# A two-layer transformer on one core: input loads on separate semaphores, and query stacks loaded from ScalarE's queue

## The chip, the cores and the metric

One Trainium2 chip; the program runs on one core. The engines are TensorE (PE in the profile), VectorE (DVE), ScalarE (ACT), GpSimd (POOL) and SyncE (SP), which only issues DMAs here. The metric is the device time of one execution in microseconds. The profile's span leaves out what lies before its first and after its last instruction.

## What is computed

x is 4 batches of 512 tokens with 128 features. Four blocks follow each other, each with a layer norm of x ahead of it and its result added to x:

```
x = x + attention0(layernorm(x))   # 16 heads of 8; low-rank q and kv projections; rotary part added
x = x + layers(layernorm(x))       # 6 layers of windowed attention (16 heads of 64, window 32) and a gated FFN
x = x + attention1(layernorm(x))   # 16 heads of 8; rotary
x = x + experts(layernorm(x))      # top-1 of 16 experts, capacity 160
```

Both attentions are full softmax over 512 keys for each of 16 heads and 4 batches, in float32 precision: queries and keys are split into three bfloat16 parts (high, middle, low), and one matmul over 48 rows of such parts gives a product of float32 accuracy.

## The kernel before

The program is written engine by engine: each engine has its own list of instructions, and semaphores order them. A wait stops all that is behind it on its engine. `LOADED` is 16 for each load counted by `ld_c`.

**Inputs.** SP issues `ident` and x (L411, L412, semaphore `ld_x`), and then in a loop (L413, L414) nine constants and four weights, all counted by `ld_c`: `mean_w`, the rope tables (512 KB each), the rotary tables of the layers, the two masks, `moe_c`, `upper`, `packed`, `packed_low`, the bias columns and `gate_t`. TensorE transposes x (L655), ScalarE copies it to `xT` (L1248), and all three of TensorE, ScalarE and VectorE then wait for the full count of `ld_c` (L657, L1249, L1540). VectorE copies the masks to bfloat16 (L1542, L1543), and sets `tick` (L1546), for which the first mean waits through `step_done`.

**Opening of an attention** (`attention(a)` of each engine, a is 0 or 1). For batches 0 and 1: mean by a matmul (L295), centring (L1444), squares (L1141), variance (L673), root (L315, L317), scaling (L1451), and then the projections (L687; 9 in attention 0, 5 in attention 1), evicted by ScalarE (L1163, L1156). The rotary step with its split in parts (`rope`, L338 to L356) is VectorE's for the queries of batch 0 and GpSimd's for the rest. The batches are opened in the order 0, 1, 3, 2.

**Stacks.** The parts lie with one head's feature in a partition, and the matmul wants them stacked in 48 partitions. So SP stores the six parts of a batch to DRAM (`write_parts`, L457, 128 KB each, semaphore `a_scr`) and loads them back in groups (`load_stacks`, L474, semaphore `a_stk` for each half): for keys and for queries, for each of two row halves r of the array, three groups, in rows of 4 KB (the four head pairs of a half):

```
GROUPS = [[(0, 0, 1, 3), (24, 1, 2, 1), (40, 1, 1, 1)], [(0, 0, 3, 1), (24, 0, 1, 2), (40, 1, 1, 1)]]
```

A group is (row, first part, parts, copies), for queries and for keys. Its DMA writes 24, 16 or 8 partitions of 4 KB, 96, 64 or 32 KB, and its source has the outer size 3, 2, or 8 (where count and copies are one). A half is 12 DMAs (`STACKED`), a batch 24. Batches 0 and 1 are loaded in the opening, 2 and 3 in the rounds. A load's DMAs start when the batch's stores have landed.

**First maxima.** `first_maxima` runs 64 score matmuls for batch 0 (L702, wants the stacks of half 0 first), each reduced by VectorE (L1459), with the means, variances and projections of batches 3 and then 2 written in between. The negated maxima of a batch are transposed (L741), copied (L1194) and moved as three more rows to the stacks by SP (`move_maxima`, L484), behind the stores of batches 3 and 2. After that come the rounds: scores with maxima (L716), exponent (L1176), weighing (L731), and the maxima of the next batch.

## Time and profile before

| | us |
|---|---|
| median of 3 timed runs | 2797.43 |
| lowest and highest of them | 2789.22, 2798.4 |
| the profiled execution, its own time | 2800.44 |
| its span | 2798.6 |
| TensorE, VectorE, ScalarE, GpSimd busy | 2209.3, 1968.2, 1508.8, 1491.8 |

The profiled execution took 1.8 us more than its span, and it is 3.0 us above the median of the timed ones. The opening of attention 0 lasts from the start to about 145 us, its rounds follow; the six layers run until about 2200, attention 1 opens at 2215, and the experts end the program.

The columns of the timeline are: start, duration (of the whole stretch, where several instructions are merged: x16), engine, line, operation, output and inputs, and in brackets how long the engine had been idle before and what ended that. SPq rows are DMA issues on SP's queue.

### The profile page before, as it was taken

How to read it: one execution, taken by the hardware profiler on the slowest of the kernel's cores; microseconds unless marked ns; L12 is line 12 of the kernel's file. 1: busy time of each engine (PE TensorE's matmuls, PEld its weight loads, DVE VectorE, ACT ScalarE, POOL GpSimd, SP SyncE). 2: the span in 40 equal slices, each digit the busy share in tenths (PEclk: the TensorE clock that was granted, in tenths of full speed). 3: DMA queues.
4: the chain of work that ended last, by engine and by line, in shares of the span. 5: the costliest groups of instructions: out<-in, count | busy, mean ns of one | idle time of the engine just before them, and what ended most of it. 6: DMA issues, size and time to landing. Idle time of an engine off the chain costs nothing.

```text
span 2798.6 us, 53907 instructions
## 1 busy us (share of the span) xinstructions
PE 2209.3 (79%) x21780; PEld 1179.8 (42%) x21780; DVE 1968.2 (70%) x2087; ACT 1508.8 (54%) x1863; POOL 1491.8 (53%) x1031
## 2 busy tenths in 40 slices
PE   4678867898898899888989898889898656787253
PEld 1111124555555555555555555555555211112253
DVE  2666628889888888888888888888886256762101
ACT  2255554666666666666666666666665313556000
POOL 5500017877776777777767767777774152000202
PEclk7688887999999999999999999999999757989586
DMA  4100000000000000100010001000000020000122
GB/s 153 51 18 24 13 1 2 16 2 17 2 10 18 17 2 2 26 17 1 2 26 3 16 2 26 2 17 2 9 2 2 4 79 13 24 24 16 51 70 67
DMA packets 55828, 59.08 MB, mean 21 GB/s; under 512 B 13142, under 2 KB 45012, under 8 KB 55508
## 3 DMA queue, kind: packets, MB, share of 16 engines
q1 hardware_dynamic: 53444, 50.77, 6.0%
q0 software_dynamic: 2128, 4.72, 0.7%
q8 instruction: 182, 2.98, 0.4%
q14 instruction: 74, 0.61, 0.1%
HBM read 44.07 MB, written 11.01 MB: 20 GB/s over the span
## 4 chain that ended last, share of the span: by engine, by line
PE 36%; POOL 18%; issue 18%; DVE 16%; ACT 8%; DMA 2%; SPq 1%; POOLq 0%; ACTq 0%; DVEq 0%
PE bank L731 5%; PE bank L702 4%; PE bank L855 4%; PE bank L919 4%; DVE big L1459 4%; POOL big L576 3%; POOL big L593 3%; PE bank L929 3%; POOL big L577 3%; POOL small L586 3%; DVE big L1565 2%; ACT big L1176 2%; ACT pxs L1301 2%; PE bank L898 1%; DVE small L1559 1%
## 5 line engine op out<-in xcount | busy, mean ns | idle before, releaser
L1459 DVE TENSOR_REDUCE big<-bank 128x1 f32<-128x512 f32 x512 | 328.5, 685 | 208.9 <-PE bank L702 204.3
L598 POOL TENSOR_TENSOR sc<-sc,small 128x1024 f32<-128x1024 f32 x96 | 263.4, 2744 | 366.6 <-DVE small L1601 366.6
L855 PE MATMUL bank<-wqk,xs 128*128 128x512 f32 x768 | 361.5, 613 | 13.0 <-ACT xs L1257 8.3
L929 PE MATMUL bank<-pxs,mw 128*128 128x256 f32 x1536 | 365.6, 381 | 0.0
L1292 ACT ACTIVATE sc<-sc 128x1024 f32<-128x1024 f32 x96 | 101.5, 1057 | 465.4 <-DVE sc L1591 465.3
L929 PEld LDWEIGHTS bank<-pxs,mw 128*128 128x128 f32 x1536 | 290.5, 192 | 101.2 <-issue 70.6
L1176 ACT ACTIVATE big<-bank 128x1024 f32<-128x1024 f32 x256 | 250.1, 1026 | 140.8 <-PE bank L716 138.4
L1565 DVE TENSOR_TENSOR big<-big,rotCl 128x2048 f32<-128x2048 f32 x96 | 226.4, 2358 | 79.3 <-POOL big L577 79.3
L702 PE MATMUL bank<-pxs 48*128 48x512 bf16 x512 | 189.2, 456 | 114.3 <-DVE big L1459 71.4
L1559 DVE TENSOR_REDUCE small<-big 128x32 f32<-128x2048 f32 x96 | 219.0, 2281 | 40.5 <-ACT big L1270 31.1
L1580 DVE TENSOR_TENSOR big<-big,small 128x1024 f32<-128x1024 f32 x192 | 245.1, 1277 | 1.1 <-POOL small L588 1.1
L919 PE MATMUL bank<-sc,xnat 32*128 32x512 f32 x1536 | 204.8, 648 | 43.6 <-ACT big L1262 40.9
L576 POOL TENSOR_TENSOR big<-big,rotSl 128x1024 f32<-128x1024 f32 x96 | 227.6, 2370 | 9.1 <-ACT big L1262 9.0
L577 POOL TENSOR_TENSOR big<-big,rotSl 128x1024 f32<-128x1024 f32 x96 | 227.5, 2370 | 0.0
L593 POOL TENSOR_TENSOR big<-big 128x1024 f32<-128x1024 f32 x96 | 226.3, 2358 | 0.0
L855 PEld LDWEIGHTS bank<-wqk,xs 128*128 128x128 f32 x768 | 140.3, 192 | 165.5 <-issue 157.3
L1301 ACT ACTIVATE pxs<-bank 128x1024 f32<-128x1024 f32 x192 | 185.6, 1019 | 25.9 <-PE bank L919 22.5
L702 PEld LDWEIGHTS bank<-pxs 48*128 48x128 bf16 x512 | 40.8, 95 | 363.5 <-DVE big L1459 265.8
L1270 ACT ACTIVATE big<-big 128x2048 f32<-128x2048 f32 x96 | 183.3, 1910 | 11.5 <-DVE small L1560 1.1
L1262 ACT ACTIVATE big<-bank 128x1024 f32<-128x1024 f32 x192 | 184.7, 1011 | 5.9 <-PE bank L855 5.9
L716 PE MATMUL bank<-pxs 56*128 56x512 bf16 x512 | 122.9, 425 | 57.0 <-DMA pxs<-big 31.8
L898 PE MATMUL bank<-kbuf,qT 64*32 64x64 f32 x12288 | 145.8, 226 | 17.3 <-issue 13.8
(236 smaller groups left out, 4012.8 us busy)
## 6 DMA issues: line engine op xcount, KB each, us to landing
wqk<-in_L_ffn_w SPq DMA_DIRECT2D x32, 256.0 KB, 3.1
wqk<-in_L_ffn_Wqkv SPq DMA_DIRECT2D x12, 512.0 KB, 4.4
pxs<-part_rows SPq DMA_DIRECT2D x64, 96.0 KB
pxs<-part_rows SPq DMA_DIRECT2D x64, 64.0 KB
wvt<-in_wv_layers_t SPq DMA_DIRECT2D x6, 512.0 KB, 4.6
wol<-in_L_ffn_Wo SPq DMA_DIRECT2D x6, 512.0 KB, 5.7
part_rows<-big SPq DMA_DIRECT2D x24, 128.0 KB
part_rows<-sc SPq DMA_DIRECT2D x24, 128.0 KB
```

Source lines behind the costliest of these rows:

```text
L576: pool.tensor_tensor(r4[:, :, :, 0:h], q4[:, :, :, h:], tab[:, :, :, 0:h], ALU.mult).then_inc(l_rb, 1)
L577: pool.tensor_tensor(r4[:, :, :, h:], q4[:, :, :, 0:h], tab[:, :, :, h:], ALU.mult).then_inc(l_rb, 1)
L593: pool.tensor_tensor(raws(i)[:, INNER:], raws(i)[:, INNER:], rotB[:, INNER:], ALU.add).then_inc(l_ak, 1)
L598: pool.tensor_tensor(p3, p3, rden(i).unsqueeze(2).broadcast_to([P, LH, 64]), ALU.mult).then_inc(l_pn, 1)
L702: pe.matmul(bank[:, 4 + r, :], qst[64 * r:64 * r + MAX_ROW, b % 2, p, qt * P:(qt + 1) * P], kst[64 * r:64 * r + MAX_ROW, b % 2, p, :], sta ...
L855: m = pe.matmul(bank[:, 2 - 2 * half + c, :], xs[:, b % 2, WIN + i * P:WIN + (i + 1) * P], wqk[:, (2 * half + c) * 512:(2 * half + c + 1) ...
L919: m = pe.matmul(bank[:, (4, 5, 2, 3)[w], :], xnat[32 * w:32 * w + 32, i % 2, half, :], p4[32 * w:32 * w + 32, :, half, :], start=(half == ...
L929: m = pe.matmul(bank[:, 6, part * 2 * P:(part + 1) * 2 * P], mw[:, 2 * (a % 4) + s, a // 4, :], pxs[:, part, a, s, :], start=(a == 0 and s ...
L1176: act.activation(pT[:, u % 2, 2 * half:2 * half + 2, :], bank[:, q:q + 2, :], ACT.Exp).then_inc(a_p, 1)
L1459: dve.tensor_reduce(nm[:, qt, 2 * p + r:2 * p + r + 1], bank[:, 4 + r, :], AX.X, ALU.max, negate=True).then_inc(a_mx, 1)
L1559: ch.link(dve.tensor_reduce(ss, sq.rearrange("p (h d) -> p h d", d=LD), AX.X, ALU.add))
L1565: dve.tensor_tensor(r4, r4, rotCl[:, i % TILES, :].rearrange("p (a d) -> p a d", a=2).unsqueeze(2).broadcast_to([P, 2, LH, LD]), ALU.mult) ...
```

## The change

- The loads get semaphores of their own in order of use: `ld_m` for `mean_w`, `ld_r` for the rope tables, `ld_a` for the first weights (`packed`, `packed_low`, bias columns), and `ld_c` for the other seven. Each engine waits for what it reads next.
- The first weights are issued by ScalarE, ahead of its activation table load. SP issues `mean_w`, the rope tables, and the other seven behind x.
- The masks land in `big` instead of `sc`; VectorE copies them after its rope of batch 0, not before the first mean.
- The 12 DMAs with the queries of batch 0 (six for each half) are issued by ScalarE after its evictions of batches 0 and 1, in both attentions; SP issues the 12 with the keys. The other batches stay on SP.

```diff
-        ld_x, ld_c = sem("ld_x"), sem("ld_c")
+        ld_x, ld_m, ld_a, ld_r, ld_c = sem("ld_x"), sem("ld_m"), sem("ld_a"), sem("ld_r"), sem("ld_c")
...
+        rope_loads = [(ropeC[:, :, :], I["c_ropeC"]), (ropeS[:, :, :], I["c_ropeS"])]
+        first_weights = [(packed[:, :], I["packed"]), (packed_low[:, :], I["packed_low"]), (bias[:, :], I["bias_columns"])]
...
+        later_loads = [
+            (mask_f[:, 0:256], I["c_maskw"]), (mask_f[:, 256:768], I["c_maskr"]),
+            (rotC[:, :, :], I["c_rotC"]), (rotS[:, :, :], I["c_rotS"]), (moe_c[:, :, :], I["c_moe"]),
+            (upper[:, :], I["c_upper"]), (gw, I["gate_t"]),
+        ]
...
+        def stack_rows(eng, b, half, which):
+
+            c, w = 4 * half * SEQ, 4 * SEQ
+            for r in range(2):
+                for row, first, count, copies in GROUPS[which]:
+                    src = part_rows[b, which, first:first + count, r, :, c:c + w]
+                    if copies > 1:
+                        src = src.broadcast_to([copies, AD, w])
+                    o, at = 64 * r + row, (b % 2) * PAIRS_A * SEQ + c
+                    eng.dma_start((qrow, krow)[which][o:o + AD * count * copies, at:at + w], src).then_inc(a_stk[b % 2][half], 16)
...
-            for dst, src in const_loads + weight_loads:
+            sp.dma_start(mean_w[:, :], I["c_mean"]).then_inc(ld_m, 16)
+            for dst, src in rope_loads:
+                sp.dma_start(dst, src).then_inc(ld_r, 16)
+            for dst, src in later_loads:
                 sp.dma_start(dst, src).then_inc(ld_c, 16)
...
+                for which in ((1, 0) if b else (1,)):
+                    stack_rows(sp, b, half, which)
...
+                if a == 0:
+                    pool.wait_ge(ld_r, 16 * len(rope_loads))
                 rope(pool, chp, a, 0, 1, (sA, sB, sC))
...
-            pe.wait_ge(ld_c, LOADED)
+            pe.wait_ge(ld_m, 16)
             pe.wait_ge(x_in, BATCH)
...
+                if a == 0 and n == 0:
+                    pe.wait_ge(ld_a, 16 * len(first_weights))
...
             attention(0)
-
+            pe.wait_ge(ld_c, LOADED)
             norm_all_tensor(pe, SEED)
...
+                act.wait_ge(zeros_set, 2 * a + 1)
+                act.wait_ge(a_scr[0], WRITTEN * (2 * a + 1))
+                for half in range(2):
+                    stack_rows(act, 0, half, 0)
                 squares_in(a, 3)
...
+            for dst, src in first_weights:
+                act.dma_start(dst, src).then_inc(ld_a, 16)
             act.preload_act_table_set("natural_log_exp_and_others")
...
-            act.wait_ge(ld_c, LOADED)
             act.wait_ge(init, 5)
+            act.wait_ge(ld_a, 16 * len(first_weights))
             attention(0)
...
+                if a == 0:
+                    dve.wait_ge(ld_r, 16 * len(rope_loads))
                 rope(dve, chd, a, 0, 0, (tA, tB, tC))
+                if a == 0:
+                    dve.wait_ge(ld_c, LOADED)
+                    dve.tensor_copy(maskw[:, :, :].rearrange("p a t -> p (a t)"), mask_f[:, 0:256]).then_inc(masks_set, 1)
+                    dve.tensor_copy(maskr[:, :], mask_f[:, 256:768]).then_inc(masks_set, 1)
...
-            dve.wait_ge(ld_c, LOADED)
             dve.wait_ge(x_in, BATCH)
-            dve.tensor_copy(maskw[:, :, :].rearrange("p a t -> p (a t)"), mask_f[:, 0:256]).then_inc(masks_set, 1)
-            dve.tensor_copy(maskr[:, :], mask_f[:, 256:768]).then_inc(masks_set, 1)
```

## Rows read from the trace of the kernel before

**Rows 1.** The page, section 1: busy us (share) xinstructions of each engine.

```profile
PE 2209.3 (79%) x21780; PEld 1179.8 (42%) x21780; DVE 1968.2 (70%) x2087; ACT 1508.8 (54%) x1863; POOL 1491.8 (53%) x1031
```

**Rows 2.** The chain of waits, 0 to 66 us: start, us, what.

```profile
9.90 6.82 DMA small<-in_gate_t
...
17.51 0.07 DVE tick L1546
...
17.71 2.06 PE bank L295 x2
...
47.73 2.93 DMA part_rows<-big
...
57.80 6.64 DMA pxs<-part_rows
...
64.48 0.60 PE bank L702
```

**Rows 3.** The timeline, 0 to 90 us.

```profile
8.03 3.68 PE L655 MATMUL bank<-ident,big 128*128 128x128 f32 x16 [8.03 <-DMA big<-in_L_attn_x]
...
11.74 0.60 ACT L1248 ACTIVATE xT<-bank 128x512 f32<-128x512 f32 x1 [0.26 <-PE bank L655]
...
26.69 1.10 PE L673 MATMUL bank<-rotSl,mean_w 128*128 128x512 f32 x2 [1.53 <-ACT rotSl L1141]
...
27.72 1.93 PE L687 MATMUL bank<-xc,packed 128*64 128x512 f32 x4
...
65.13 0.69 DVE L1459 TENSOR_REDUCE big<-bank 128x1 f32<-128x512 f32 x1 [22.24 <-PE bank L702]
...
68.98 0.63 ACT L1141 ACTIVATE sqn<-xc 128x512 f32<-128x512 f32 x1 [23.37 <-DVE xc L1444]
...
78.05 1.97 PE L687 MATMUL bank<-xc,packed 128*64 128x512 f32 x2
...
87.36 1.13 PE L687 MATMUL bank<-xc,packed 128*128 128x512 f32 x2
```

**Rows 4.** The timeline, 84 to 120 us, GpSimd's rows.

```profile
87.84 1.26 POOL L338 TENSOR_TENSOR sc<-big,ropeC 128x512 f32<-128x512 f32 x1 [20.54 <-ACT big L1163]
...
118.60 1.26 POOL L338 TENSOR_TENSOR sc<-kbuf,ropeC 128x512 f32<-128x512 f32 x1 [10.64 <-ACT kbuf L1163]
```

**Rows 5.** DMA issues, 0 to 130 us: KB each, us from issue to landing.

```profile
packed<-in_packed SPq DMA_DIRECT2D x1, 640.0 KB, 7.3
...
packed_low<-in_packed_low SPq DMA_DIRECT2D x1, 160.0 KB, 7.3
```

**Rows 6.** Windows of the start: busy us per engine, TensorE's clock, DMA share, GB/s.

```profile
2.00:3.00 1.00, 0.00 (x0) 0.00 (x0) 0.00 (x0) 0.02 (x1) 1.00 (x1) 1.00 0.09 25
...
4.00:5.00 1.00, 0.00 (x0) 0.00 (x0) 0.00 (x0) 0.00 (x0) 1.00 (x1) 1.00 0.99 340
...
9.00:10.00 1.00, 1.00 (x6) 1.00 (x5) 0.00 (x0) 0.60 (x1) 1.00 (x3) 1.00 1.02 403
```

**Rows 7.** The timeline of SP's queue, 0 to 140 us.

```profile
50.68 14.98 SPq L474 DMA_DIRECT2D pxs<-part_rows  x24
65.72 6.52 SPq L457 DMA_DIRECT2D part_rows<-sc  x6
```

**Rows 8.** Windows between changes of the granted clock.

```profile
15.80:25.50 9.70, 5.83 (x6) 1.67 (x6) 1.68 (x5) 1.95 (x3) 0.00 (x0) 0.50 1.03 348
25.50:46.40 20.90, 18.14 (x50) 7.34 (x50) 10.89 (x12) 13.94 (x21) 9.39 (x8) 0.99 0.21 47
```

**Rows 9.** The chain of waits in the opening of attention 1.

```profile
2258.87 6.57 DMA pxs<-part_rows
```

**Rows 10.** Windows of the load of the stacks of batch 0.

```profile
52.20:64.40 12.20, 0.00 (x0) 0.00 (x0) 0.00 (x0) 0.00 (x0) 11.43 (x12) 0.50 0.21 78
...
74.00:79.00 5.00, 4.03 (x8) 0.79 (x7) 4.55 (x8) 0.00 (x0) 0.00 (x0) 0.50 0.14 50
```

**Rows 11.** Waits of SP's queue, 0 to 200 us: us in total, times, longest.

```profile
SPq L474 <- DMA part_rows<-sc: 6.8, 1, 6.8
```

More of the change, by code:

```diff
@@ L149, in build @@
         rotB, sq = big[:, 2, :], big[:, 3, :]
+        mask_f = big[:, 3, 1024:1792]
         sc = sb("sc", [P, 4, 1024])
-        mask_f = sc[:, 0, 0:768]
         small = sb("small", [P, 8, 32])
@@ L385, in norm_all_vector @@
             dve.sem_inc(ln_out, BATCH)
-        const_loads = [
-            (mean_w[:, :], I["c_mean"]), (ropeC[:, :, :], I["c_ropeC"]), (ropeS[:, :, :], I["c_ropeS"]),
-            (rotC[:, :, :], I["c_rotC"]), (rotS[:, :, :], I["c_rotS"]),
-            (mask_f[:, 0:256], I["c_maskw"]), (mask_f[:, 256:768], I["c_maskr"]), (moe_c[:, :, :], I["c_moe"]),
-            (upper[:, :], I["c_upper"]),
-        ]
+        rope_loads = [(ropeC[:, :, :], I["c_ropeC"]), (ropeS[:, :, :], I["c_ropeS"])]
+        first_weights = [(packed[:, :], I["packed"]), (packed_low[:, :], I["packed_low"]), (bias[:, :], I["bias_columns"])]
         gw = small[:, 7, NE:2 * NE]
         three_halves = small[:, 7, 0:1]
-        weight_loads = [
-            (packed[:, :], I["packed"]), (packed_low[:, :], I["packed_low"]), (bias[:, :], I["bias_columns"]),
-            (gw, I["gate_t"]),
+        later_loads = [
+            (mask_f[:, 0:256], I["c_maskw"]), (mask_f[:, 256:768], I["c_maskr"]),
+            (rotC[:, :, :], I["c_rotC"]), (rotS[:, :, :], I["c_rotS"]), (moe_c[:, :, :], I["c_moe"]),
+            (upper[:, :], I["c_upper"]), (gw, I["gate_t"]),
         ]
         xrows = I["L0_attn_x"].rearrange("a (c p) d -> p (a c) d", p=P)
-        LOADED = 16 * (len(const_loads) + len(weight_loads))
+        LOADED = 16 * len(later_loads)
         SEED, LAYER0, ATT1, MOE0 = BATCH, 2 * BATCH, (2 + DEPTH) * BATCH, (3 + DEPTH) * BATCH
@@ L465, in load_stacks @@
                     sp.wait_ge(a_st, (n - 2) * PAIRQ + (half + 1) * PAIRQ // 2)
-                c, w = 4 * half * SEQ, 4 * SEQ
-                for which in (1, 0):
-                    for r in range(2):
-                        for row, first, count, copies in GROUPS[which]:
-                            src = part_rows[b, which, first:first + count, r, :, c:c + w]
-                            if copies > 1:
-                                src = src.broadcast_to([copies, AD, w])
-                            o, at = 64 * r + row, (b % 2) * PAIRS_A * SEQ + c
-                            sp.dma_start((qrow, krow)[which][o:o + AD * count * copies, at:at + w], src).then_inc(a_stk[b % 2][half], 16)
+                for which in ((1, 0) if b else (1,)):
+                    stack_rows(sp, b, half, which)
             def move_maxima(a, b, half):
@@ L1538, in attention @@
                 residual_of(a, BATCH - 1, 5)
-            dve.wait_ge(ld_c, LOADED)
             dve.wait_ge(x_in, BATCH)
-            dve.tensor_copy(maskw[:, :, :].rearrange("p a t -> p (a t)"), mask_f[:, 0:256]).then_inc(masks_set, 1)
-            dve.tensor_copy(maskr[:, :], mask_f[:, 256:768]).then_inc(masks_set, 1)
             dve.wait_ge(init, 5)
-            dve.wait_ge(masks_set, 2)
             dve.memset(tick[:, :], 0.0).then_inc(step_done, 1)
```

## The prediction

> **What bounds the kernel now.** I read the page first: TensorE is busy for 79% of 2798.6 us and no engine for more [rows 1], and the diff touches neither the six layers nor the rounds of the attentions. Everything must therefore come out of the two openings. Next I read the chain of waits of the first 66 us [rows 2]. It has two stretches in which nothing computes. The first ends with the load of `gate_t`, the thirteenth of the loads that share `ld_c`: it lands at 9.90 + 6.82 = 16.72, the two mask copies follow until 17.5, and TensorE begins the first mean at 17.71. The second is the store of `part_rows` and the load of the stacks: from the store's last issue at 47.73 to 64.48 TensorE and VectorE have nothing. The timeline says what was ready by then [rows 3]: x's last copy to `xT` ended at 11.74 + 0.60 = 12.34.
>
> A shift of the opening is kept. GpSimd waits for the projections of batch 3 (20.54 us) and again for those of batch 2 (10.64 us) [rows 4]. These projections are written between the first maxima, and the maxima of batch 0 are moved on SP's queue only behind the stores that follow them, so each later step hangs on the first maxima. I read nothing there with a fixed start.
>
> **Part 1, the input semaphores.** Removed from the path: the wait for all 13 loads and the masks' copies. With x landing as now, the step behind 12.34 is the `tick` memset and the hop to TensorE, 17.71 - 17.51 = 0.20 [rows 2], and about 0.1 for the wake-up: TensorE would begin at 12.65 instead of 17.71, a gain of 5.06.
>
> What is late next is x itself. It lands at 8.02 (the first transpose starts there [rows 3]), and nothing of the change makes it earlier. The three weight loads (640 and 160 KB [rows 5], and 8 KB of bias columns: 827 kB) now go out from ScalarE's queue at once, before x. The windows show how much room there is: before 3 us the DMA engines are busy for 0.09 only, and from 4 us on they are full at 340 GB/s [rows 6]. x's bytes begin in between, at some 3.1 us. If the weights start about 1 us after their issue, at 1.7 us, (3.1 - 1.7) x 340 = 480 kB are through before x begins, and the remaining 350 kB share the engines with it: 1.0 us. The bounds are 0 (they wait for x) and 827/340 = 2.4 us (all ahead of it). I take 1.2, a little over the worked value since the issue of x may be held up too. Gain: 5.06 - 1.2 = 3.9.
>
> On arbitration, the Trainium skill (page "DMA: Bandwidth & Descriptors", section "Queues, rings and completion order") says that each DMA engine takes turns between its queues packet by packet. By that x is slowed only while weights are left, which would give the 1.0 us; no row of this trace has two busy queues.
>
> The other edits of this part are hidden. `mean_w` (64 KB) is the next load behind x on SP, so it lands just behind it, and it is wanted at about 13.8, after x has been transposed. The weights are wanted at the first projection, 27.72 - 4 us [rows 3], the rope tables later still, and all 13 loads together land by 16.72 now. The masks' copies fall to VectorE after its rope, in a hole of 22.24 us [rows 3]; without that hole they would cost the 0.8 us from 16.72 to 17.51. The three issues on ScalarE (at the stacks' 0.62 us each, 1.9 [rows 7]) and the activation table behind them have until x is transposed, after 8.02. SP's queue loses three issues ahead of the stores of zeros and the layer's weights, which nothing in the opening waits for.
>
> **TensorE's clock.** From 15.8 to 25.5 the granted clock is 0.50, the 1.2 GHz level, after TensorE had stood still from 11.7 to 17.7; from 25.5 to 46.4 it is 0.99 [rows 8]. In the slow stretch a pair of these matmuls takes 2.06 us [rows 2], afterwards 1.10 [rows 3]. Three pairs lie on the path there, so 0 to 2.9 us come back if the shorter stop keeps the clock up. The mean to variance chain still has stops of some 1.5 us, so I count 1.0.
>
> **Part 2, stacks from two queues.** Half 0 of batch 0 is 12 DMAs. Before, SP issues the 24 of both halves in 14.98 us, 0.62 each [rows 7]; the twelfth goes out at 57.80 and lands 6.64 later. The sixth store of `part_rows` needs 2.93 for the same way [rows 2]. After, each queue issues six for half 0, so the last goes out at 50.68 + 5 x 0.62 = 53.8. If a queue were the limit, it would land 2.93 later, at 56.7: a gain of 64.44 - 56.7 = 7.7 us, in each attention. In the second one the same row says 6.57 [rows 9].
>
> But 6.64 is not 2.93: 3.7 us of backlog have grown already, so the transfers are slower than the issue. The windows say why [rows 6, 10]. In 52.2 to 64.4, 78 GB/s move at a busy share of 0.21, which is 3.4 of 16 engines at 23 GB/s each. In the bulk loads, 403 GB/s at 1.02 are 25 GB/s for each engine. So the engines that have work go at nearly the full rate, and few have work. The clearest row is 74 to 79 us: SP has issued nothing since 65.72 + 6.52 = 72.24 [rows 7], and still 50 GB/s flow at 0.14, which is 2.2 engines with 22 GB/s each; the last store of batch 1 waits behind them, 6.8 us from its issue to its landing [rows 11]. Two or three engines carry the tail of these loads, whatever the others have finished. The DMAs of a group carry 24, 16 and 8 rows of 4 KB, in patterns whose outer sizes are 3, 2 and 8. A second queue feeds the same engines, and the bytes of half 0 before the wait are the same. So I count 0.
>
> The Trainium skill, same page, section "Why a DMA increments its semaphore by 16 and not by 1", gives the split: the largest number up to 16 that divides the outer sizes of both sides, on the lowest-numbered engines. That makes 3, 2 and 8 engines here, so that engines 0 and 1 get 32 + 32 + 4 KB of each 192; four such groups are 278 kB, at 22 GB/s 12.6 us, from 52.2 to 64.8. The trace's 64.44 agrees.
>
> Bounds of part 2: +7.7 for each attention, and -1. The loss comes if ScalarE's issues lag: then key DMAs of half 1 on SP get in among the queries of half 0, by about the lag, one or two issues of 0.62 us. A small gain (to 2 us) is possible where one queue left engines short: 23 against 25 GB/s is 8% of 12.2, 1 us.
>
> On ScalarE 12 issues run from 50.68 to about 58.2 or, if the two queues hinder each other, 65.7. Its next instruction is the `Square` of batch 3, which starts at 68.98 after a wait of 23.37 [rows 3], and behind it the evictions for batches 3 and 2. The cover is 3 us at worst; gone, the Square and the variance matmul behind it would slip with it. SP is free after 12 issues rather than 24 (58.2, not 65.7), which lets the query stores of batch 1 go earlier. The key stores still wait for GpSimd, and the stacks of batch 1 for the same engines; they are first wanted in the round of batch 0, behind all the first maxima.
>
> **Sum.** 3.9 + 1.0 + 0 + 0 = 4.9 us. Against the profiled execution's own time, 2800.44, that is 2795.5. That execution is 3.0 above the median of the three timed runs (2797.43), and I set the forecast by the median: **2792.5**. What a measurement can tell here is about 0.3%, or 8.4 us; the runs of before themselves lie 9 us apart. So the likeliest verdict is "no difference".
>
> **Rivals.**
> - *The queue is the limit.* Half 0 lands at about 56.7 less the shift, in both attentions: 2797.4 - 4.9 - 15.4 = 2777. For it: SP issues without a pause through the load, and no row shows two queues at once. Against it: the flow after the last issue. Half an effect (2785) lies in it. Chance 0.14.
> - *The start is given back.* x comes 2.4 us later, and the clock falls where it now stands at 1.00; gain 2.7 or less, 2795 to 2798. For it: weights are issued before x. Against: the idle engines before 3 us. Chance 0.15.
> - *Slower: the projections run at 1.2 GHz.* Those of the first two batches now lie at 0.99 [rows 8]. One projection takes 1.97 us at the low level and 1.13 at the high one [rows 3], 0.84 more. Eight lie on the way to GpSimd's rope and 14 among the first maxima of batches 3 and 2: 22 x 0.84 = 18.5 us, so 2797.4 - 3.9 + 18.5 = 2812. It decides from (3.9 + 8.4)/0.84, 15 of the 22. For it: at 0.50 TensorE was already busy for 5.83 of 9.70 us before the clock rose. Against: it rose within 8 us of its first matmul there. Chance 0.05.
>
> **How the numbers follow.** The forecast has 0.66. Its own range is 2797.4 - (5.1 + 2.9 + 2 x 2) = 2785 to 2797.4 - (2.7 - 2) + 2 for the scatter of the runs = 2799. For 8 in 10 I go to 2781 on the fast side, into half the queue rival, and to 2801 on the slow one. Faster than 2789 are nearly all of the queue rival (0.13), and about a fifth of the forecast's, where the clock and the small gains add up (0.15): 0.28. Slower than 2806: 0.05. The rest, 0.67, is the same.
>
> **What would show it.** In the changed profile: x landing between 8.0 and 10.4, at 9.2 by my count; the first mean at 12.7 to 15.1, at about 13.8; no wait on `gate_t`; the mask casts after the rope. From the first issue of the stacks to the first maximum, 50.68 to 64.48, 13.8 us now, should stay 13 to 14.8 in both attentions, though the issues end some 4 us earlier; the flow at 50 GB/s and the landing of the batch 1 stores should stay. If the 13.8 falls to 6 or 8, I was wrong on the engines. If the mean begins before 13 and the total is not lower, the shift is lost behind, to the clock most likely.

## The result, and the profile after

The changed kernel takes 2806.0 us (median of 15 runs, 2795.1 to 2815.0) against 2793.6 of before measured beside it (15 runs): ratio 1.0043, 95% interval 1.0030 to 1.0056. The forecast was 2792.5 with a range of 2781 to 2801; the kernel is slower, by more than what the measurement can tell from no change. Its profiled execution took 2798.95 us, span 2797.1.

The opening did get faster, only less. In the chain of waits of the kernel after (start, us, what), in the rows that answer to [rows 2]:

```profile
1.36 8.53 DMA big<-in_L_attn_x
...
14.31 0.07 DVE tick L1562
...
14.52 1.11 PE bank L295 x2
...
43.63 3.05 DMA part_rows<-big
...
50.99 11.02 DMA pxs<-part_rows
62.05 0.60 PE bank L710
```

`gate_t` is gone from it, the first mean starts at 14.52 instead of 17.71 and the first maximum at 62.05 instead of 64.48. Between them stands a worse number: the last issue that the first maximum waits for now goes out at 50.99, not at 57.80, but lands 11.02 us later, not 6.64.

The timeline of the two queues, SP's (SPq) and ScalarE's (ACTq), answers to [rows 7] and shows what is issued next to x:

```profile
1.36 0.89 SPq L420 DMA_DIRECT2D big<-in_L_attn_x  x1
2.31 3.84 SPq L421 DMA_DIRECT2D mean_w<-in_c_mean  x1
...
46.70 7.56 SPq L415 DMA_DIRECT2D pxs<-part_rows  x12
54.31 14.90 SPq L468 DMA_DIRECT2D part_rows<-sc  x6
```
```profile
0.75 0.43 ACTq L1258 DMA_DIRECT2D packed<-in_packed  x1
1.21 0.57 ACTq L1258 DMA_DIRECT2D packed_low<-in_packed_low  x1
1.81 0.59 ACTq L1258 DMA_DIRECT2D bias<-in_bias_columns  x1
...
46.76 8.49 ACTq L415 DMA_DIRECT2D pxs<-part_rows  x12
66.55 0.63 ACT L1149 ACTIVATE sqn<-xc 128x512 f32<-128x512 f32 x1 [25.38 <-DVE xc L1458]
```

Windows of the same kernel, for [rows 6, 8, 10] (busy us per engine, TensorE's clock, DMA share, GB/s):

```profile
2.00:3.00 1.00, 0.00 (x0) 0.00 (x0) 0.00 (x0) 0.57 (x1) 1.00 (x1) 1.00 0.69 207
4.00:5.00 1.00, 0.00 (x0) 0.00 (x0) 0.00 (x0) 0.00 (x0) 1.00 (x1) 1.00 0.81 278
...
14.50:23.20 8.70, 5.53 (x8) 1.55 (x8) 1.98 (x3) 2.58 (x4) 0.00 (x0) 0.80 1.01 319
52.00:64.00 12.00, 1.95 (x3) 0.60 (x3) 0.69 (x1) 0.00 (x0) 10.59 (x11) 0.50 0.30 105
72.00:74.00 2.00, 1.63 (x4) 0.31 (x3) 1.90 (x4) 0.00 (x0) 0.00 (x0) 0.50 0.14 48
```

Between 2 and 3 us, where 25 GB/s moved, 207 move now, most of them weights. The DMA queues from 3 to 5 us (packets, MB, packet times as a share of the 16 engines' time; q1 is SP's queue, q10 ScalarE's), first before, then after:

```profile
q1 hardware_dynamic: 231, 0.47, 90.4%
```
```profile
q10 hardware_dynamic: 186, 0.65, 83.8%
q1 hardware_dynamic: 58, 0.04, 8.9%
```

While the weights move, SP's queue, with `ident` and x, moves next to nothing; nearly all of the 827 kB of weights are through at 5 us in this trace, and x's packets follow. While the stacks load, 105 GB/s move instead of 78, and still the first half lands no sooner: what is added is not half 0. The second opening repeats it, in its chain of waits (before, [rows 9]: 6.57):

```profile
2247.48 11.44 DMA pxs<-part_rows
2258.91 0.05 issue
2258.96 0.61 PE bank L710
```

Two things outside the openings differ too. One is idle time of TensorE in the layers. The page's groups of costliest instructions (busy, mean ns | idle before) have the layers' projections, at line 855 before and 863 after, which the diff does not touch. First before, then after:

```profile
L855 PE MATMUL bank<-wqk,xs 128*128 128x512 f32 x768 | 361.5, 613 | 13.0 <-ACT xs L1257 8.3
```
```profile
L863 PE MATMUL bank<-wqk,xs 128*128 128x512 f32 x768 | 359.6, 611 | 15.2 <-ACT xs L1271 8.3
```

The idle time ahead of them is 2.2 us longer. It lies at the heads of the iterations of the layer loop (where an iteration's first projections begin). TensorE's timeline of one such place, before and after:

```profile
1351.34 0.70 PE L855 MATMUL bank<-wqk,xs 128*128 128x512 f32 x1
1352.85 3.16 PE L855 MATMUL bank<-wqk,xs 128*128 128x512 f32 x7 [0.81 <-issue]
```
```profile
1338.79 1.15 PE L906 MATMUL bank<-kbuf,qT 64*32 64x64 f32 x94
1341.31 3.59 PE L863 MATMUL bank<-wqk,xs 128*128 128x512 f32 x8 [1.37 <-issue]
```

"Issue" says that nothing which the profile follows releases the matmul. Of such gaps ahead of these matmuls, counted from 0.3 us on, before has six of 0.5 to 1.0 us, 4.5 in all, and after five of 1.2 to 1.4 us, 6.5 in all: the first of the six, 0.8 us, is gone, and the five later ones are 0.6 us longer on average. (The expectations below give 4.1 to 4.6 us for before; by this count it is 4.5, and 4.6 for before again.) The two rows above show what the 0.6 us are: before does one matmul of the iteration (0.70 us) ahead of its gap, and after does none. The other thing is the clock: the mean granted clock of the runs of after is lower, which the experiments return to.

### The profile page after: what moved, and what is told of

Its sections match the earlier page's. It is cut to its first block, busy times and chain, and to the rows that moved or that the text cites. A ratio compares the mean times of both kernels' runs of the same rounds, so it can differ in the third digit from the quotient of the medians.

```text
span 2797.1 us, 53815 instructions
## 1 busy us (share of the span) xinstructions
PE 2195.0 (78%) x21684; PEld 1181.5 (42%) x21780; DVE 1969.4 (70%) x2087; ACT 1510.2 (54%) x1863; POOL 1492.7 (53%) x1031
## 4 chain that ended last, share of the span: by engine, by line
PE 38%; issue 17%; DVE 16%; POOL 16%; ACT 9%; DMA 2%; SPq 1%; ACTq 0%; POOLq 0%; DVEq 0%
PE bank L739 5%; PE bank L710 4%; PE bank L863 4%; PE bank L927 4%; PE bank L937 4%; DVE big L1473 3%; POOL big L582 3%; POOL big L599 3%; POOL big L583 3%; DVE big L1581 2%; POOL small L592 2%; ACT big L1184 2%; ACT pxs L1315 2%; PE bank L906 2%; DVE small L1575 2%
## 5 line engine op out<-in xcount | busy, mean ns | idle before, releaser
L863 PE MATMUL bank<-wqk,xs 128*128 128x512 f32 x768 | 359.6, 611 | 15.2 <-ACT xs L1271 8.3
L710 PE MATMUL bank<-pxs 48*128 48x512 bf16 x512 | 183.5, 438 | 119.6 <-DVE big L1473 73.0
L724 PE MATMUL bank<-pxs 56*128 56x512 bf16 x512 | 116.2, 405 | 58.3 <-DMA pxs<-big 32.4
L906 PE MATMUL bank<-kbuf,qT 64*32 64x64 f32 x12288 | 145.6, 226 | 19.1 <-issue 15.7
```

What stands on the lines that cost most here:

```text
L710: pe.matmul(bank[:, 4 + r, :], qst[64 * r:64 * r + MAX_ROW, b % 2, p, qt * P:(qt + 1) * P], kst[64 * r:64 * r + MAX_ROW, b % 2, p, :], sta ...
L863: m = pe.matmul(bank[:, 2 - 2 * half + c, :], xs[:, b % 2, WIN + i * P:WIN + (i + 1) * P], wqk[:, (2 * half + c) * 512:(2 * half + c + 1) ...
```

## The experiments

Every kernel ran beside the kernel before on the same chip; the sets below ran on four chips. Much of the time of a single run follows its mean granted clock, and that scatters from run to run. So beside the ratio I give a second number: a straight line through all 299 runs, one common slope and one level for each kernel, gives 1.53 us less for each 0.001 of mean clock, and leaves a scatter of 3.4 us. "At 0.903" is a kernel's level on that line, with a standard error of 1 us for 12 runs. The kernel before has 2797.4 there (134 runs, the 12 of "before again" among them). That error is not all: the four sets of before have 2795.5 to 2798.3, and before again, with no edit, has 2799.3, 1.9 over the 2797.4. So a level that differs by 2 us shows nothing by itself.

| kernel | runs | median us | ratio to before, 95% interval | mean clock | at 0.903 |
|---|---|---|---|---|---|
| before again | 12 | 2797.3 | 1.0007 (0.9989 to 1.0026) | 0.9042 | 2799.3 |
| after | 15 | 2806.0 | 1.0043 (1.0030 to 1.0056) | 0.9013 | 2802.3 |
| after, again | 6 | 2810.4 | 1.0055 (1.0035 to 1.0076) | 0.8993 | 2804.5 |
| after, third | 12 | 2803.4 | 1.0043 (1.0023 to 1.0063) | 0.9026 | 2801.8 |
| part 1 only | 12 | 2799.0 | 1.0014 (0.9992 to 1.0036) | 0.9021 | 2798.1 |
| part 2 only | 12 | 2803.7 | 1.0030 (1.0007 to 1.0053) | 0.9021 | 2802.4 |
| two instructions more | 12 | 2799.7 | 1.0001 (0.9986 to 1.0017) | 0.9035 | 2799.8 |
| part 1, same length | 12 | 2795.2 | 0.9991 (0.9978 to 1.0005) | 0.9034 | 2795.8 |
| half 1 later | 12 | 2799.5 | 1.0006 (0.9991 to 1.0021) | 0.9035 | 2800.4 |
| pieces of 8, two queues | 12 | 2798.0 | 1.0006 (0.9988 to 1.0024) | 0.9045 | 2799.1 |
| pieces of 8, one queue | 12 | 2795.2 | 1.0002 (0.9980 to 1.0024) | 0.9008 | 2791.4 |
| part 1, weights behind x | 12 | 2789.2 | 0.9984 (0.9961 to 1.0006) | 0.9041 | 2791.8 |
| the same, pieces of 8, two queues | 12 | 2787.1 | 0.9976 (0.9957 to 0.9995) | 0.9058 | 2791.8 |
| the same, pieces of 8, one queue | 12 | 2784.8 | 0.9974 (0.9950 to 0.9998) | 0.9034 | 2785.5 |
| stacks by ScalarE alone | 12 | 2794.3 | 1.0007 (0.9982 to 1.0031) | 0.9041 | 2797.3 |

Four numbers are read from each profile by the same rows: when x lands (TensorE's first transpose starts), the first mean, and from the first issue of the stacks to the first maximum, in attention 0 and in attention 1.

| kernel | x lands | first mean | attention 0 | attention 1 |
|---|---|---|---|---|
| before, before again | 8.03, 8.00 | 17.71, 17.29 | 13.8, 14.1 | 13.7, 13.7 |
| after (three profiles) | 9.94, 10.47, 10.32 | 14.52, 15.05, 14.89 | 15.3, 15.7, 15.2 | 15.3, 16.5, 15.9 |
| part 1 only | 10.53 | 15.11 | 13.7 | 13.8 |
| part 2 only | 7.90 | 17.32 | 15.3 | 15.5 |
| two instructions more | 8.06 | 17.51 | 13.8 | 13.7 |
| part 1, same length | 9.96 | 14.54 | 13.9 | 13.9 |
| half 1 later | 8.04 | 17.38 | 14.0 | 14.3 |
| pieces of 8, two queues | 10.19 | 14.77 | 13.2 | 13.4 |
| pieces of 8, one queue | 7.86 | 17.24 | 9.8 | 10.4 |
| part 1, weights behind x | 7.89 | 12.32 | 13.9 | 14.1 |
| the same, pieces of 8, two queues | 8.18 | 12.76 | 13.5 | 13.8 |
| the same, pieces of 8, one queue | 7.97 | 12.35 | 9.9 | 10.5 |
| stacks by ScalarE alone | 8.00 | 17.63 | 14.7 | 15.4 |

**Before against itself, and after again.** Neither has an edit.

> The kernel before, unchanged, timed against itself. The two profiles at hand differ by 1.6 us, the medians of 15 runs by 12.5, so part of the loss may be scatter of TensorE's granted clock from run to run. If it is scatter between programs or occasions, this run moves away from the kernel before by several us; if the loss belongs to the change, it stays within 0.3% and its ratio near 1.000.

> The changed kernel again, on one chip with its parts. If the loss belongs to the program: 1.003 to 1.006 again, some 2806. If it was the occasion: 1.000 or below, as the opening's 3.9 us shift would give (2790).

Before against itself is 1.0007, so the loss is none of the comparison's, and after shows it again with 1.0055.

**Part 1 only.** The stacks stay on SP as before; the semaphores, the order of the loads and the weights from ScalarE are the change's.

> The inputs' semaphores and ScalarE's issue of the first weights, all stacks from SP. Shown by the profile after: first mean at 14.5 instead of 17.7, first projection 4.45 us earlier. Theory A, the loss is part 2's: faster than before by 4 to 6 us (2788 to 2790). Theory B, the loss comes with the shift of the opening against something with a period or place of its own (the clock): slower like the whole change (2800 to 2806).

**Part 2 only.** The loads are those of before.

```diff
-                for which in (1, 0):
+                for which in ((1, 0) if b else (1,)):
                     stack_rows(sp, b, half, which)
...
+                for half in range(2):
+                    stack_rows(act, 0, half, 0)
```

> Only the queries' stacks of batch 0 from ScalarE's queue in both attentions, inputs as before. The profile after shows 15.3 us from the first issue to the first maximum against 13.8, so 1.5 us lost in each attention: 2796 to 2797 by that alone. Theory A, the loss is part 2's and lies further on: 2804 or more. Theory B: 2793 to 2797.

At 0.903 part 1 costs 0.7 us, which is not told from nothing, and part 2 costs 5.0; together 5.7, and the three sets of after average 2802.5, 5.1 over before. The parts add within the error. Of the expectations, both theories on part 1 missed (it neither gains its 4 to 6 us nor loses like the whole change), and part 2 came out at the theory that its loss is more than the 3 us of its two stack loads: those explain 1.5 and 1.8 of the 5.0. In the profile each part has its own mark: the late x with part 1 alone, the 15.3 us with part 2 alone. And the gaps at the heads of the layer loop sum to 7.0 us with part 1 and to 5.1 with part 2: the row of the projections has 15.5 us idle with part 1 and 13.6 with part 2. That points at something in part 1 which reaches the layers.

**Two instructions more.** Part 1 makes TensorE's program two instructions longer ahead of the layer loop: one wait ahead of the first projection, one behind the attention. Here before has just two such waits, both long reached:

```diff
+                if a == 0 and n == 0:
+                    pe.wait_ge(ld_c, LOADED)
...
             attention(0)
+            pe.wait_ge(ld_c, LOADED)
             norm_all_tensor(pe, SEED)
```

> The kernel before, with two instructions more in TensorE's program and nothing else: two waits on semaphores that have long been reached, one ahead of the first projection and one between the attention and the layers, where part 1 has its two. Theory (TensorE stands longer at the head of each of the five iterations of the layer loop because its program has moved by two instructions): its idle time without a cause ahead of the five first matmuls is 6.5 to 7 us in all, 1.3 to 1.4 us each, as with part 1, against 4.1 to 4.6 us before, and the stretch from the first layer to the second attention is 2 to 3 us longer than the 1814.8 to 1816.9 us of before; at an equal mean clock the time is 2 to 3 us over before's. Rival (the stall comes from the shift of the start, or from the semaphores of the loads): 4.1 to 4.6 us and no change.

The gaps were 6.5 us in all, the projections' row had 15.0 us idle, the stretch from the first layer to the second attention took 1818.9 us against 1816.9 and 1814.8, and at 0.903 the kernel stands 2.4 us over before (1.5 over the runs of before beside it). The ratio, 1.0001, shows nothing of it, and the stretch is a weak witness: after, third, with the gaps of after (6.2 us), has 1811.6 us there, at a granted clock of 0.966, the highest of all the profiles in that stretch. What carries the reading are the gaps. TensorE's timeline of this kernel at one loop head, with nothing of the change in it:

```profile
1063.77 0.43 PE L900 MATMUL bank<-kbuf,qT 64*32 64x64 f32 x21
1065.92 3.59 PE L857 MATMUL bank<-wqk,xs 128*128 128x512 f32 x8 [1.72 <-issue]
```

**Part 1, same length.** The reverse: the two waits are left out of TensorE's program, since what ScalarE and VectorE wait for ahead of it covers them.

```diff
-                if a == 0 and n == 0:
-                    pe.wait_ge(ld_a, 16 * len(first_weights))
...
             attention(0)
-            pe.wait_ge(ld_c, LOADED)
```

> Part 1 alone, written so that TensorE's program keeps its length: the two waits that part 1 adds there (for the packed weights, for the late constants) are left out, since ScalarE and VectorE wait for the same loads ahead of it. Theory (moved program): the idle time ahead of the five first matmuls of the layer loop is back at 4.1 to 4.6 us, the stretch from the first layer to the second attention at 1814.8 to 1816.9 us; the opening keeps the gain of part 1 (first mean near 15.1 us, first maximum near 61 us against 64), so that at an equal mean clock the time is 2 to 3 us under before's, where part 1 as it was stands at before's. Rival (the stall belongs to the loads): 7 us again, and a time equal to before's at an equal clock.

The opening is unchanged (14.54), the stretch of the layers takes 1814.7 us, and at 0.903 the kernel is 1.6 us under before and 2.3 under part 1 as it was: the expected sign, a little small, and near the error of the levels. The gaps sum to 5.4 us, less than 7.0 but above the expected 4.6. Over all 16 profiles the idle time in the projections' row falls into two groups without an overlap: 14.9 to 15.8 us in the six whose TensorE program is two longer, 12.7 to 14.0 in the ten others, this one's the highest (the gaps: 6.2 to 7.3 against 3.9 to 5.4). The row of this kernel in the page:

```profile
L861 PE MATMUL bank<-wqk,xs 128*128 128x512 f32 x768 | 362.3, 614 | 14.0 <-ACT xs L1265 8.4
```

The traces also hold the loading of the program's own instructions, in packets of 16 KB on a queue of its own. For the loop head of after shown above (DMA queues, 1335 to 1343 us):

```profile
q8 instruction: 1, 0.02, 0.7%
```

With all 16 traces there are 89 such gaps from 0.3 us on. At each, exactly one of these packets starts, 0.5 to 2.0 us before TensorE goes idle, and the matmul behind the gap begins 1.2 to 1.6 us after the packet's end. (The layers have some 150 such packets, one in 11 us on average, so this is hardly chance; most have no gap behind them.) In the six longer programs all 30 gaps lie ahead of the first matmul of an iteration's projections; in the ten others 49 lie behind it, so that about 0.6 us of work is done first, and the other 10 are the gap that the longer programs do not have. So these gaps end with a load of instructions, and the two waits in front move the place in the loop at which the engine has to stop for it. That it is the position, and not something else about two waits, was not tested with other lengths.

**Half 1 later.** Part 2 with the second half issued, on both queues, only when the first has landed:

```diff
+                if b == 0 and half == 1:
+                    sp.wait_ge(a_stk[0][0], STACKED * (2 * a + 1))
...
-                for half in range(2):
-                    stack_rows(act, 0, half, 0)
+                stack_rows(act, 0, 0, 0)
+                act.wait_ge(a_stk[0][0], STACKED * (2 * a + 1))
+                stack_rows(act, 0, 1, 0)
```

> Part 2 alone, with the second half of the first stacks issued, on both queues, only when the first half has landed. Theory A (on two queues the second half's transfers, which SP issues while ScalarE's are still moving, sit between those of the first half on the same two or three engines): from the first issue to the first maximum pass 13.8 us or less instead of 15.3 us, and the 1.5 us per attention come back; the second half lands later, near 26 us after the first issue, and what waits for it may lose as much. Theory B (ScalarE's queue itself is slower: its issues run at 0.72 us each, the last at 4.3 us, and its transfers take longer to land): 15 to 15.5 us again.

It was 14.0 and 14.3 us: 1.2 us each of the 1.5 and 1.8 come back, most of it, as the first theory has it. Half 0 alone on two queues takes about as long as on one. Its rows:

```profile
50.02 18.24 SPq L418 DMA_DIRECT2D pxs<-part_rows  x12
68.30 6.71 SPq L468 DMA_DIRECT2D part_rows<-sc  x5
```
```profile
64.03 0.60 PE L708 MATMUL bank<-pxs 48*128 48x512 bf16 x1 [19.71 <-DMA pxs<-part_rows]
```

Held back by its wait, SP also issues the stores of batch 1 only from 68.30, as before ([rows 7]: 65.72). With the change they begin at 54.31, 8 us ahead of the landing of half 0. So this run holds back half 1 and the stores together, and does not say which of them costs how much. Nor does it give the whole loss of part 2 back: its level, 2800.4, is 2.0 us under part 2's and still 3.0 over before.

**Stacks by ScalarE alone.** In part 2 only, SP's share is ScalarE's too:

```diff
-                for which in ((1, 0) if b else (1,)):
+                for which in ((1, 0) if b else ()):
...
                 for half in range(2):
-                    stack_rows(act, 0, half, 0)
+                    for which in (1, 0):
+                        stack_rows(act, 0, half, which)
```

> The kernel before with the first batch's stacks of both attentions issued by ScalarE's queue alone, keys and queries, in the transfers of before. Theory A (it is two queues moving at once that costs, whichever they are): from the first issue to the first maximum 13.5 to 14.2 us, as with SP alone. Theory B (ScalarE's queue is the slower one: 0.72 us for an issue there against 0.62 us on SP): 12 issues at 0.72 us and as late as that a landing, 15 us or more, and the last issues of half 1 end 17.3 us after the first instead of 15.0.

It was 14.7 and 15.4 us, between the two theories in the first attention and with the second in the other. It does not tell them apart, because SP is left free: it issues the stores of batch 1 from 57.73 (in the second attention from 2245.78, 5 us after the stacks' first issue), so two queues move at once here too. ScalarE's 24 issues take 15.97 us, 0.67 each, against 0.62 on SP.

```profile
50.71 15.97 ACTq L418 DMA_DIRECT2D pxs<-part_rows  x24
```
```profile
57.73 10.79 SPq L468 DMA_DIRECT2D part_rows<-sc  x6
```

**Pieces of 8 rows, two queues.** The whole change, with the stacks of the first batch moved in pieces of 8 rows, none broadcast; 24 transfers of 32 KB per half instead of 12 (TensorE's wait counts them accordingly):

```diff
+            if b == 0:
+                for r in range(2):
+                    for row, part in ROWS8[which]:
+                        eng.dma_start((qrow, krow)[which][64 * r + row:64 * r + row + AD, c:c + w],
+                                      part_rows[0, which, part, r, :, c:c + w]).then_inc(a_stk[0][half], 16)
+                return
```

> The whole change, and the first batch's stacks of both attentions moved in pieces of 8 rows, none broadcast: 12 transfers per half in each queue as before, or 24 in all, but each with its own descriptors over more engines. Theory of the prediction (the transfers are limited by the two or three DMA engines that a broadcast transfer sits on, not by the queue's issue): the flow while half 0 moves rises well over the 40 to 50 GB/s seen so far, and from the first issue to the first maximum pass 8.5 to 11 us where it was 15.3 us with the change; each attention gives back 4 to 6 us, so that the time is 8 to 12 us under the changed kernel's at an equal clock, some 3 to 7 us under before's. Rival (the time is in the latency of the scratch and in the issue, whatever the engines): 13.5 to 15.3 us, and nothing gained.

The 13.2 and 13.4 us are 2 to 2.5 us better than after, not 4 to 6; that is nearer to the rival. At 0.903 the kernel is 3.4 us under after, not 8 to 12.

**Pieces of 8 rows, one queue.** The same pieces in the kernel before, all on SP:

> The kernel before with the first batch's stacks moved in pieces of 8 rows, all 24 of a half issued by SP alone. On two queues this flowed at 72 to 82 GB/s, one piece of 32 KB every 0.42 us over both queues, and took 13.2 us from the first issue to the first maximum. Theory A (that rate is a bound of the engines or of the memory, whatever the queue): 24 pieces at 0.42 us and some 3 us until the last is landed and waited for, 13 to 14 us again, the time equal to before's at an equal clock. Theory B (the rate is one piece every 0.84 us for each queue): 40 GB/s, 24 x 0.84 = 20 us and 3, 22 to 24 us from the first issue to the first maximum, 8 to 10 us lost in each attention, the time 16 to 20 us over before's.

Neither theory foresaw it: 9.8 and 10.4 us, faster than anything on two queues. The ratio is 1.0002, as its runs fell at a low mean clock (0.9008); at 0.903 it is 6.0 us under before. Windows from 52 to 58 us, first this kernel, then the one with two queues:

```profile
52.00:58.00 6.00, 0.00 (x0) 0.00 (x0) 0.00 (x0) 0.00 (x0) 5.70 (x6) 0.50 0.37 94
```
```profile
52.00:58.00 6.00, 0.00 (x0) 0.00 (x0) 0.00 (x0) 0.00 (x0) 5.66 (x6) 0.50 0.53 77
```

One queue: 94 GB/s, with packet times that add up to a share of 0.37, 5.9 of the 16 engines. Two queues: 77 GB/s at 0.53, 8.5 engines. The same pieces from the same scratch, and their packets take longer when two queues feed them; whether they then move or wait, the share does not say. The stores of batch 1, which SP issues from 56.32 on with two queues, are not the cause: from 52 to 56 us, ahead of them, it is 93 GB/s at 0.36 against 76 at 0.51. On one queue the limit is the issue, by its row in the timeline (48 pieces in 16.98 us, 0.354 each, and 24 x 0.354 = 8.5 of the 9.8 us):

```profile
49.96 16.98 SPq L420 DMA_DIRECT2D pxs<-part_rows  x48
```

By the split rule of the Trainium skill (page "DMA: Bandwidth & Descriptors", section "Why a DMA increments its semaphore by 16 and not by 1") pieces of 8 rows go to 8 engines. The shares, 5.9 engines on one queue and 8.5 on two, do not contradict it, but they do not show which engines carried the pieces.

**Part 1, weights behind x.** Part 1 at the old length of TensorE's program, with the weights on SP:

```diff
-            for dst, src in first_weights:
-                act.dma_start(dst, src).then_inc(ld_a, 16)
...
             sp.dma_start(mean_w[:, :], I["c_mean"]).then_inc(ld_m, 16)
+            for dst, src in first_weights:
+                sp.dma_start(dst, src).then_inc(ld_a, 16)
```

> Part 1 with TensorE's program at its old length, and with the three packed weights issued from SP's queue right behind x and mean_w, none from ScalarE's. Theory (the weights of the second queue share the engines with x and delay it by 1.9 us): x lands near 8.0 us again and the first mean starts near 12.7 to 13.3 us, 1.3 to 1.8 us earlier than the 14.5 us of the same kernel with ScalarE's queue; the weights land near 14 us, ahead of the first projection at 22.5 us. The start gains 1.3 to 1.8 us more and the time at an equal clock is 3 to 4 us under before's. Rival (x waits for something else, or the constants behind it hold the start): x at 9.9 us again, the first mean at 14.5 us. Second rival (mean_w, now with the weights close behind it, lands later and takes x's place): the first mean near 14 us.

x lands at 7.89 and the first mean starts at 12.32, somewhat better than expected and 2.2 us ahead of the same kernel with ScalarE's queue. TensorE's timeline:

```profile
7.89 3.52 PE L663 MATMUL bank<-ident,big 128*128 128x128 f32 x16 [7.89 <-DMA big<-in_L_attn_x]
12.32 1.10 PE L295 MATMUL bank<-xT,mean_w 128*128 128x512 f32 x2 [0.91 <-DVE tick L1556]
```

At 0.903 it is 5.6 us under before, more than the expected 3 to 4, and 4.0 under the same with ScalarE's queue, where the start alone explains 2.2. Its ratio, 0.9984 (0.9961 to 1.0006), does not exclude no change.

**The two versions that the runs point to.** The last kernel with the pieces of 8 rows, on two queues and on SP alone.

> The version that the runs so far point to: separate semaphores in order of use, the packed weights from SP behind x, TensorE's program at its old length, and the first stacks of both attentions in pieces of 8 rows on two queues. Theory (the gains add: 4.5 us of the start, 0.4 to 1.4 us in each attention, nothing at the layer loop): at an equal clock 4 to 7 us under before's and 9 to 12 us under the changed kernel's. Rival (what is gained at the start is lost in a wait further on): no more than 2 us under before's.

> The earlier start (separate semaphores in order of use, the packed weights from SP behind x, TensorE's program at its old length) with the first stacks in pieces of 8 rows, all issued by SP: nothing of the change's second queue is left. Theory (the two gains are at different places and add: 4 to 6 us of the start, 4.0 us in the first attention and 2.8 us in the second): the first maximum near 54 to 55 us, attention 1 to its first maximum in 47.5 us, and at an equal clock 10 to 12 us under the kernel before. Rival (the earlier maxima of batch 0 only wait longer for something later, and the gain of the stacks is given back): 4 to 6 us under before, as with the start alone.

On two queues the pieces add nothing to the start (2791.8 at 0.903, both); on one they add 6.3 us: 2785.5, 11.9 under before (10.0 under the runs of before beside it). The ratio, 0.9974 (0.9950 to 0.9998), lies just clear of no change, and against after, which ran beside it a third time, the medians are 2784.8 and 2803.4, 0.993. In this kernel's chain of waits the stack's stretch is the issue itself, and the last landing comes 2.10 us behind:

```profile
41.37 2.94 DMA part_rows<-big
...
52.08 2.10 DMA pxs<-part_rows
54.23 0.61 PE bank L721
```

**After, a third time,** for its clock.

> The whole change again, for its mean granted clock: 0.901 and 0.899 in two sets of runs against 0.903 to 0.904 of before, which is 4 us of the loss at the 1.5 us that 0.001 of the mean clock costs over all runs. Theory A (the change lowers the clock): 0.899 to 0.902 again, and a time of 2802 to 2810 us. Theory B (the sets of runs scatter by 0.001 each, and those two fell low): near 0.903 to 0.904, and a time of 2800 to 2804 us, the cost of the stages alone.

The clock was 0.9026, between the two theories, against 0.9049 of the runs of before beside it. All 33 runs of after have 0.9014 (standard error 0.0006), the 134 of before 0.9040 (0.0004): 0.0026 lower, which at 1.53 us for 0.001 is 4.0 us, plus or minus some 1.1. The first two sets may have been low by chance in part; the difference stays. With it the loss comes to 5.1 + 4.0 = 9.1 us, less than the 12 us of the first ratio: the 15 runs of before measured there have a median of 2793.6, some 3 us under three of the four later sets, and no clock on record. Against the runs of before beside it, after's level is 7.3 us over (again) and 6.3 us over (third), so the loss at equal clock is known as 5 to 7 us.

## Why the prediction was wrong

- **x is late (1.2 us in the sum): right kind, too small.** x lands 1.9 us later, 1.9 to 2.5 in the six profiles with weights on ScalarE's queue, so near the upper bound of 2.4 that I had given to "all ahead of it". I had let the weights run alone until x came, and then share with it; but from 3 to 5 us ScalarE's queue moved 0.65 MB and SP's 0.04, and SP's issue of `mean_w` is held for 3.84 us. In front of x on SP's queue is also `ident`, 64 KB, which the sum left out. Shown by putting the weights behind x: 7.89. By the turns packet by packet of the Trainium skill (page "DMA: Bandwidth & Descriptors", section "Queues, rings and completion order") the delay was to be 1.0 us, an estimate. The trace does not show equal turns, if a packet of the profile is one of that page: from 3 to 5 us it has 186 of one queue to 58 of the other, and x is delayed by about all of the other queue's bytes. Why the share was so unequal is not shown.
- **The start:** the first mean moved by 3.2 us instead of 3.9, as x did (2.2 to 3.2 over all the profiles of the two kernels). So the rival that gives the start back was half right, on x. **The clock there:** right in the profile above, and partly by luck. From the first mean to the first projection pass 8.75 instead of 10.01 us, 1.3 against the 1.0 that I counted; the granted clock is 0.80 there, against 0.50 in the stretch that answers to it [rows 8]. After, third, has 8.93, but after, again, has 9.83, and before again 9.63: in that profile of after the first mean still runs at the low level, as it does in four of the nine profiles with an earlier start (2.04 or 2.05 us; 1.10 in the other five):

```profile
15.05 2.04 PE L295 MATMUL bank<-xT,mean_w 128*128 128x512 f32 x2 [0.90 <-DVE tick L1562]
```

- **"A shift of the opening is kept": right inside attention 0, as far as there is one.** GpSimd's two waits end at 84.54 and 114.67, 3.3 and 3.9 us earlier than in [rows 4], and at 84.65 and 114.74 in after, third. In after, again, where the clock did not rise earlier, they end at 87.29 and 118.10, no earlier than in before again (86.92 and 117.25).
- **"A second queue feeds the same engines ... I count 0": this step failed.** Right was the half of it that dismissed a gain: half 0 alone on two queues takes 14.0 us, and the flow of 48 GB/s in the tail stays. Wrong was that nothing would be lost. The stacks take 15.2 to 15.7 us in attention 0 and 15.3 to 16.5 in attention 1: on average 1.5 and 2.2 us lost, beyond the bound of 1 for each. I had named the way it can come, key transfers of half 1 among the queries of half 0, and tied it to a lag of ScalarE's issues. No lag was needed: a queue with half the issues is done sooner, and what it sends next, half 1 and then the stores of batch 1, shares the engines with half 0. Holding both back returns 1.2 of the 1.5. I had read "SP is free earlier" as a cover, and it was the cost.
- **"The diff touches neither the six layers nor the rounds", so everything must come out of the openings: this failed too.** Two waits more in TensorE's program lengthen five loop heads by some 0.6 us each and remove the first gap, about 2 us in all by the gaps and by the projections' idle time (the levels at 0.903 say 2.4 and 2.3, with an error of over 1). Shown both ways, by adding only them and by leaving only them out. The term was put at nothing because none of the layers' lines is in the diff; the gaps end with loads of the program's instructions, and what stands ahead of the loop moves the place where they fall.
- **The slower rival (projections at 1.2 GHz)** did not come. It was the wrong mechanism for the right side.

Against the 4.9 us of gain that I forecast, after stands 5.1 us over before at equal clock. Placed by the means of the profiles: the first maximum of attention 0 comes 1.5 us earlier, the loop heads of the layers lose about 2, the stacks of attention 1 lose 2.2. That makes 2.7 us lost; the rest, 2.4, has no place, and part 2, which alone stands 5.0 over before with 3.3 in its stacks, has a rest of its own. Further 4 us go with the lower mean clock. Part 1 and part 2 alone have 0.9021 each, and the other variants 0.9034 to 0.9058 except the single queue in pieces of 8 with 0.9008, so no part can be named as the cause. Both the rest and the clock stay open, and together they are more than what was placed. The forecast also started from 2797.4, the median of three runs, where the 15 runs of before beside after had 2793.6.

## What to carry to other kernels

Order the first loads by use on one queue, and put on a second one only what may go ahead of what is waited for: here 827 kB on the second queue delayed x by nearly their whole time. Before a load is split over two queues, look at the flow and the busy share while it moves: if few engines carry it, change the pieces of the transfers, and expect that the freed queue sends its next work in among what is waited for. For gains of some microseconds compare an untouched loop's idle time as well; here two waits in front of it cost 2 us, as much as the edit gave.

## What was not expected of the hardware

- The idle time at a loop's head without any releaser depends on two instructions ahead of it in TensorE's program: 3.9 to 5.4 us over the whole loop in ten profiles, 6.2 to 7.3 in six. Each of the 89 gaps ends 1.2 to 1.6 us after the end of one 16 KB packet of instructions.
- Two queues moved equal pieces of 32 KB at 77 GB/s with a busy share of 0.53, one queue at 94 GB/s with 0.37.
- Three loads of 827 kB on a second queue, issued from 0.75 us on, delayed a load issued at 1.36 us by 1.9 to 2.5 us, and the issue of the next one on the first queue took 3.84 us instead of 2.06.
- The runs of one kernel in one set span 11 to 38 us, and about three quarters of that scatter (of its variance) goes with the mean granted clock, at 1.53 us for 0.001.
